# Causal attention in a Mamba and mixture-of-experts block: row maxima interleaved 20 steps ahead and placed per block of 512 queries

## The reference

```python
scores = jnp.einsum('bqhd,bkhd->bhqk', q, k) / math.sqrt(hd)      # 16 heads of width 16, 2048 tokens
scores = jnp.where(causal, scores, jnp.asarray(-1000000000.0, scores.dtype))
probs = jax.nn.softmax(scores, axis=-1)
attn = jnp.einsum('bhqk,bkhd->bqhd', probs, v).reshape(Bb, Tt, d) @ Wproj
```

## Time and profile before

| | |
|---|---|
| median of 3 runs | 4642.17 us |
| the profiled execution | 4645.66 us, its span 4644.1 us |
| busy over the span: TensorE matmul, VectorE, ScalarE, GpSimd | 79%, 61%, 53%, 41% |
| granted TensorE clock, mean | 0.858 |
| before the attention stage, 0 to 2352.7 us | TensorE busy 1736.4 us, clock 0.89 |
| attention stage, 2352.7 to 3819.8 us | TensorE busy 1360.3 us, VectorE 831.7, ScalarE 684.5, GpSimd 111.5, clock 0.83 |
| after it, 3819.8 to 4644 us | TensorE busy 549.1 us, clock 0.82 |

### The profile page before, as it was taken

How to read it: one execution, slowest core, us unless ns; L and a number is a source line. 1 busy time by engine, 2 the same in 40 slices (tenths; PEclk the granted TensorE clock), 3 DMA queues, 4 the chain that set the end, 5 groups by cost and what they waited for, 6 DMA issues and landing times. The chain is left out here.

```text
span 4644.1 us, 70787 instructions
## 1 busy us (share of the span) xinstructions
PE 3645.9 (79%) x23028; PEld 2230.4 (48%) x23028; DVE 2811.0 (61%) x4386; ACT 2476.2 (53%) x3874; POOL 1905.8 (41%) x1767
## 2 busy tenths in 40 slices
PE   8477888887878878656569999999999984499990
PEld 4156666666666666544334333333333223366660
DVE  4278888888888888644557766667657005411105
ACT  3288998889888899611201555555545431111110
POOL 0078888888888888733310010000000003300006
PEclk9689999999999999877755999999979556699995
DMA  6443333333333333344440010001000004312115
GB/s 212 116 110 83 104 98 92 83 89 96 92 83 92 83 98 96 99 160 157 170 119 3 6 20 18 18 6 20 18 8 6 8 15 148 123 62 68 70 41 182
DMA packets 163298, 367.82 MB, mean 79 GB/s; under 512 B 21603, under 2 KB 68694, under 8 KB 147984
## 3 DMA queue, kind: packets, MB, share of 16 engines
q1 hardware_dynamic: 130672, 276.91, 21.5%
q0 software_dynamic: 16784, 52.10, 3.1%
q10 hardware_dynamic: 15504, 34.61, 1.9%
HBM read 263.73 MB, written 102.26 MB: 79 GB/s over the span
## 5 line engine op out<-in xcount | busy, mean ns | idle before, releaser
L506 POOL TENSOR_TENSOR scan_hC<-scan_hh,scan_cbc 128x512 f32<-128x512 f32 x1024 | 1379.7, 1374 | 160.7 <-DVE scan_hh L718 103.9
L718 DVE TENSOR_TENSOR_SCAN scan_hh<-scan_dA,scan_state,scan_bx 128x512 f32<-128x512 f32 x1024 | 1253.1, 1265 | 212.1 <-PE scan_bx L810 102.7
L1496 PE MATMUL attend_s<-attend_kt,attend_qt 32*128 32x512 f32 (+3 forms) x2560 | 825.5, 647 | 67.3 <-DVE attend_mx L1407 28.5
L810 PE MATMUL scan_bx<-kept_ident,scan_dBxT 128*128 128x128 f32 x4096 | 678.8, 292 | 197.8 <-DVE scan_hh L718 135.0
L1515 PE MATMUL attend_s<-attend_qt,attend_kt 32*128 32x512 f32 (+3 forms) x2560 | 723.8, 652 | 8.6 <-POOL attend_pb L1380 4.1
L820 PE MATMUL scan_acc<-kept_ident,scan_hC 128*128 128x128 f32 x4128 | 657.8, 287 | 53.8 <-ACT scan_uu L568 28.3
L559 ACT ACTIVATE scan_dBxT<-scan_dtxT,scan_bt 128x512 f32<-128x512 f32 x1028 | 655.6, 710 | 81.8 <-PE scan_bx L810 81.6
L810 PEld LDWEIGHTS scan_bx<-kept_ident,scan_dBxT 128*128 128x128 f32 x4096 | 503.8, 150 | 389.6 <-DVE scan_hh L718 234.6
L1407 DVE TENSOR_REDUCE attend_mx<-attend_s 128x1 f32<-128x512 f32 x768 | 495.8, 685 | 299.1 <-PE attend_s L1496 297.3
L554 ACT ACTIVATE scan_dA<-scan_dt,scan_an 128x512 f32<-128x512 f32 x1028 | 660.9, 712 | 29.1 <-DVE scan_hh L718 29.0
L1466 ACT ACTIVATE attend_pb<-attend_s 128x1024 f32<-128x1024 f32 x384 | 390.5, 1023 | 401.7 <-PE attend_s L1515 401.7
(11 more groups left out here) (202 smaller groups left out, 3895.0 us busy)
## 6 DMA issues: line engine op xcount, KB each, us to landing
scan_xs<-scratch_xin SPq DMA_DIRECT2D x288, 256.0 KB, 6.2
scan_cbc<-scratch_crows SPq DMA_DIRECT2D x64, 1024.0 KB, 4.8
scratch_y<-scan_uu ACTq DMA_DIRECT2D x17, 1024.0 KB, 4.2
mix_yf<-scratch_y SPq DMA_DIRECT2D x10, 1024.0 KB, 5.2
mix_yb<-scratch_y SPq DMA_DIRECT2D x10, 1024.0 KB, 8.8
mix_z<-scratch_sz SPq DMA_DIRECT2D x10, 1024.0 KB, 12.5
route_at<-scratch_attn SPq DMA_DIRECT2D x160, 64.0 KB, 2.3
scratch_xin<-proj_out_x SPq DMA_DIRECT2D x8, 1024.0 KB, 5.8
```

Of the source, the lines that this page charges most:

```text
L506: pool.tensor_tensor(hC[n % 2][:, m, :], h[:, m, :], rows, ALU.mult).then_inc(hc_ok, 1)
L718: dve.tensor_tensor_scan(hh[n % 2][:, m, r], dA[n % 2][:, m, r], bx[bank(j)][:, r], state[:, d, n, m:m + 1], ALU.mult, ALU.add).then_inc(h ...
L810: last = pe.transpose(bx[bank(j)][:, t * P:(t + 1) * P], dBxT[turned_slot(n)][:, t, m * P:(m + 1) * P], k["ident"][:, :])
L1496: pe.matmul(s1[v % S1][:, 0:w], qt[n % SETS][rows, t * P:(t + 1) * P], kt_[n % SETS][rows, c * C:c * C + w], start=True, stop=True).then_i ...
```

## The change

`attend` treats units and steps as two running series over all groups, the units 20 ahead (`LEAD`). So 20 units run alone at the start, then every step has one unit beside it, of its own group or the next, and the last 20 steps have none.

The units go by block of 512 queries like the steps. In each block the four crossed units stand so that, with 20 steps between, they fall beside crossed steps of equal width where the order allows: units 20-23 beside steps 0-3, units 28-31 beside steps 8-11, the next group's units 0-3 beside steps 20-23. Units 8-11 fall beside whole steps 28-31, and steps 36-39 have whole units beside them.

The maxima are reduced, turned, copied and placed after each block, a *round*: 32 in all instead of 8, each for 16 rows of `mrows` instead of 64. VectorE copies a round's rows after the unit that follows the block. TensorE turns them at the end of the iteration with that unit, once the last tile in bank `s1[0]` has been read, and waits for the copied rows before the next tile in that bank. The second pass waits for placed maxima at the start of each block. There are two sets of `qt` and `kt_` instead of three, and the load of group n + 1 stands on the SP queue between the placements of the second and third block of group n, behind a wait for the last step of group n - 1.

In the last 20 steps the scores of both pairs follow one another on TensorE, and both halves of the values come after them.

```diff
-    SETS = 3
+    SETS = 2
     PB = 3
+    LEAD = 20
...
+    units = []
+    for qc in range(NC):
+        whole = [(t, c) for t in range(JT * qc, JT * qc + JT) for c in range(qc)]
+        crossed = [(t, qc) for t in range(JT * qc + JT - 1, JT * qc - 1, -1)]
+        at = len(whole) if qc < NC - 1 else JT
+        units += whole[:at] + crossed + whole[at:]
+    assert len(units) == NSTEP
+    NUNIT = GROUPS * NSTEP
...
-        m = s.sb("m", [P, HG, KT])
-        mrows = s.sb("mrows", [HG * KT, P])
+        m = s.sb("m", [P, HG, JT])
+        mrows = s.sb("mrows", [HG * JT, P])
...
-        pm = s1[0][0:HG * KT, 0:P]
+        pm = s1[0][0:HG * JT, 0:P]
...
-            for n in range(GROUPS):
-                place_max(n)
-                if n and n + 2 < GROUPS:
-                    load(n + 2)
+            for r in range(GROUPS * NC):
+                if r % NC == 2 and r // NC + 1 < GROUPS:
+                    load(r // NC + 1)
+                place_max(r)
...
+            def block_max(u, r):
+
+                qc = r % NC
+                dve.wait_ge(s1_read, (u + 1) * HG)
+                dve.wait_ge(edge_ok, (r + 1) * JT)
+                if r:
+                    dve.wait_ge(m_turned, r)
+                dve.tensor_reduce(m[:, :, :], mx[:, :, qc * JT:qc * JT + JT, :], AX_X, ALU.max).then_inc(m_ok, 1)
...
-            for n in range(GROUPS):
-                for st in range(NSTEP):
-                    maxima(n, st)
-                split_max(n)
-                copy_rows(n)
+            for u in range(NUNIT):
+                crossings += maxima(u)
+                if round_after(u) is not None:
+                    block_max(u, round_after(u))
+                if round_after(u - 1) is not None:
+                    copy_rows(round_after(u - 1))
+            copy_rows(GROUPS * NC - 1)
...
+                    if v % S1 == 0 and turned:
+                        pe.wait_ge(m_rows, turned)
...
-            def turn_max(n):
-                pe.wait_ge(m_ok, n + 1)
+
+            def turn_max(u, r):
+
+                last = min(u + 1, NUNIT) * HG - 1
+                pe.wait_ge(s1_read, last // S1 * S1 + 1)
+                pe.wait_ge(m_ok, r + 1)
...
-                if at % NSTEP == 0 and pair == 0:
-                    pe.wait_ge(m_in, (n + 1) * HG * 16)
+                if kt == 0 and pair == 0:
+                    pe.wait_ge(m_in, (n * NC + qc + 1) * HG * 16)
...
+            turned = 0
+            for at in range(-LEAD, NUNIT):
+                u = at + LEAD
+                if at >= 0:
+                    scores2(at, 0)
+                if u < NUNIT:
+                    scores1(u, 0)
+                    if at > 0:
+                        values(at - 1, 0)
+                if at >= 0:
+                    scores2(at, 1)
+                if u < NUNIT:
+                    scores1(u, 1)
+                elif at > 0:
                     values(at - 1, 0)
...
+                if at > 0:
                     values(at - 1, 1)
...
+                if round_after(u - 1) is not None:
+                    turn_max(u, round_after(u - 1))
+                    turned += 1
```

More of the change, by code:

```diff
@@ L1388, in _, with round_after @@
                 pool.wait_ge(stored[i], 16 * GROUPS * NC // 2)
-        def tiles1(st, heads):
-            return [(t, c, h) for t, c in firsts[st] for h in heads]
+        def round_after(u):
+            if u < 0 or u >= NUNIT or u % NSTEP not in ends:
+                return None
+            return u // NSTEP * NC + ends.index(u % NSTEP)
         @block.vector
@@ L1397, in _, with maxima @@
             dve.wait_ge(mx_ok, 1)
[L1399 to L1403, removed]
+            crossings = 0
+            def maxima(u):
+                n, (t, c) = u // NSTEP, units[u % NSTEP]
+                r = n * NC + t // JT
+                if r >= NC:
+                    dve.wait_ge(m_ok, r - NC + 1)
+                own = edge[crossings % 2]
+                for i, h in enumerate((2, 3, 0, 1)):
+                    v = u * HG + i
                     bank = s1[v % S1]
@@ new lines, in maxima @@
+                    if i == 0 and crossings >= 2:
+                        dve.wait_ge(edge_ok, crossings - 1)
+                    dve.tensor_tensor(own[:, h, :], bank[:, w:w + P], cap_s[:, :], ALU.min).then_inc(s1_read, 1)
+                if c == t // JT:
+                    dve.wait_ge(s1_read, (u + 1) * HG)
+                    dve.tensor_reduce(mx[:, :, t, JT], own[:, :, :], AX_X, ALU.max).then_inc(edge_ok, 1)
+                return c == t // JT
+            def block_max(u, r):
+                qc = r % NC
+                dve.wait_ge(s1_read, (u + 1) * HG)
+                dve.wait_ge(edge_ok, (r + 1) * JT)
+                if r:
+                    dve.wait_ge(m_turned, r)
+                dve.tensor_reduce(m[:, :, :], mx[:, :, qc * JT:qc * JT + JT, :], AX_X, ALU.max).then_inc(m_ok, 1)
@@ L1481, in _, with scores1 @@
             pe.wait_ge(caps_ok, 1)
[L1483 to L1486, removed]
+            def scores1(u, part):
+                n, (t, c) = u // NSTEP, units[u % NSTEP]
+                if u % NSTEP == 0 and part == 0:
                     pe.wait_ge(loaded[n % SETS], (n // SETS + 1) * HG * 3 * 16)
[L1488 to L1491, removed]
+                w = min(C, (t + 1) * P - c * C)
+                for i, h in list(enumerate((2, 3, 0, 1)))[2 * part:2 * part + 2]:
+                    v = u * HG + i
                     rows = slice(32 * h, 32 * h + 32)
-                    w = min(C, (t + 1) * P - c * C)
                     if v >= S1:
                         pe.wait_ge(s1_read, v - S1 + 1)
+                    if v % S1 == 0 and turned:
+                        pe.wait_ge(m_rows, turned)
                     pe.matmul(s1[v % S1][:, 0:w], qt[n % SETS][rows, t * P:(t + 1) * P],
                               kt_[n % SETS][rows, c * C:c * C + w], start=True, stop=True).then_inc(s1_mm, 1)
-                    v += 1
-            def turn_max(n):
-                pe.wait_ge(m_ok, n + 1)
+            def turn_max(u, r):
+                last = min(u + 1, NUNIT) * HG - 1
+                pe.wait_ge(s1_read, last // S1 * S1 + 1)
+                pe.wait_ge(m_ok, r + 1)
                 hold(pe, k)
```

58 lines of the change are left out of this document (14 added, 44 removed).

## The result

The changed kernel takes 4419.3 us, the median of 4 executions (4410.8 to 4420.6); the kernel before, on the same chip, 4647.0 (4641.6 to 4653.6). The ratio is 0.9506, 95% interval 0.9486 to 0.9525: 5% faster. The forecast was 4445, the range 4400 to 4510. The profiled execution took 4420.6 us, its span is 4419.1, its mean granted clock 0.89.

A forecast was written before the change was run, and what follows sets the result against it. TensorE was taken to bound the middle; VectorE and TensorE alternate in the lead. Attention: -3.5 + 76 + 2 + 1096 + 66, plus 1.5, is 1238 against 1435.5 us; 4645.7 - 197.5 - 3.5 = 4445, range 4400 to 4510.

The forecast's parts named there:

- middle: The 300 attention steps with units beside them: 7.5 groups of 146.1 us, 1096 us.
- tail: Last 20 steps, without units: four heads fill four strips; 66 us, between 60 at full clock and 74 at the lower.
- Start and lead: Before the first exponential: two memsets fewer, -3.5 us; 20 units alone instead of 40, 151.3 + 2.1 becomes 76 + 2.
- Even spread: Middle: one unit per step, none with two, -9.0 us a group; units at steps 36-39 add 0 to 0.8.
- Equal widths: Middle: crossed steps beside equally wide units take 13.0 us, steps 0-3 14.8; together -1.6 us a group.
- Rounds: Middle: turning maxima four times a group adds a transpose and two TensorE waits, 1.1 us a round, +4.4 a group.
- Whole steps: Middle: expected to stay at 3.6 us; the prediction is wrong if they grow.
- Clock: Middle: drops began around steps 36-39 and cost 4.3 us a group; 3 us a group are kept.
- Hidden rounds: Rival: transposes fit into gaps (-24), last 20 steps keep full clock (-6), crossed blocks reach 12.5 (-12); 4403 us, chance 0.12.
- Costly rounds: Rival: each round costs 2.5 us (+42) and the clock loses 5 more a group (+37); 4524 us, chance 0.12.
- clock collapse: Rival: clock falls in matched narrow blocks, 15.2 us each, 23 blocks; 4773 us, slower than before, chance 0.04.
- Late placement: Rival: nothing gained from equal widths (+12) and maxima placed late (+40); 4497 us, chance 0.04.

The follow-up runs named there:

- the lead of 30: The changed kernel with the maxima pass 30 steps ahead instead of 20 (`LEAD = 30`): 4544.4 us, ratio 0.9765 to the kernel before.
- the later turn: The changed kernel with each round's transpose moved behind the first scores of the next step: 4445.3 us, ratio 0.9555 to the kernel before.
- The edit with one wait: The changed kernel with VectorE's wait for the previous group's maxima only at each block's first unit, not every unit: 4407.9 us, ratio 0.9473.
- the repeated execution: The changed kernel, nothing changed, run once more on the chip of the follow-up runs: 4419.8 us, ratio 0.9500 to the kernel before.

## Why the prediction was right, and where its sizes were off

The sum for the profiled execution was 4645.7 - 197.5 = 4448.2 us; it took 4420.6, 27.6 less: start -2, lead +1, middle -11, tail -16.

**Start and lead.** The first scores come 5.6 us earlier for 3.5; 2.0 of it had arisen before the stage, the rest is as forecast. The lead is 79.2 for 78: right. The 4.08 us wait for the placed maxima is gone, and no such wait shows anywhere. The 10 more units alone of the lead of 30 cost 38 us, the 3.8 a unit of the prediction.

**Even spread.** Right: no step holds two units. But 0 to 0.8 for units at steps 36-39 was too little: the block takes 14.5 us for 13.4 (+8 over seven groups). The row that was read for it, of the block 20-23, does not have whole units alone beside it, though the prediction says so: 12 of its 33 first-pass matmuls are narrow.

**Equal widths.** 12.6 us for 13.0 at steps 8-11 and, before the round's share, at 20-23; 13.84 for 14.8 at steps 0-3 where the clock holds: -13 in all. The term of -1.6 a group was about half of what they are worth against the earlier trace rows, and left out that unequal steps lose more when the clock is low, which the lead of 30 showed.

**Rounds.** With the equal widths the term that was sized worst in the middle: 1.1 us a round, 4.4 a group. Against the same places in a block without a round (steps 12 and 13, 3.44 + 3.66; 8 and 9, 3.50 + 3.12), the changed kernel's group 2 has +0.68 at steps 4 and 5 (3.65 + 4.13), +0.73 at 20 and 21, +0.35 at 24 and 25, and +0.84 at 32: 2.6 in this group, and 2.9 to 3.0 in groups 1 and 3 by the same reading; about -12 in all. Both waits were real, but short: TensorE idles 5.9 us before 32 transposes and 2.3 us for the copied rows, where the prediction looked for 1 us around each. A badly placed transpose is dear for another reason, that it parts two scores that would share the array, as the later turn showed. The drain at each change of mode that the Trainium skill, "TensorEngine Tiling (Array Packing)", Key Properties, asks for has no row of its own here. A kernel without rounds wasn't tried, so 2.6 to 3.0 us is a reading of the trace.

**Whole steps.** 3.65 for 3.58 beside the units of groups 1 to 7, +9 in all on the steps without a round: not in the prediction, which went through waits added on TensorE and not those on VectorE. The edit with one wait showed it. That whole steps grow was one of the prediction's signs of being wrong; they did, by 2%.

**Clock.** 3 us a group were kept; against 13.84 for steps 0-3, which the repeated execution has where the clock held, the changed kernel lost 19 us over the 300 steps, 2.5 a group: right in size, wrong in place. The prediction took them from around steps 36-39; with units beside them these steps are at 1.00, and the falls now start in steps 0 and 1, at the stall that GpSimd's queue makes. The store stood in the same place before the change, where TensorE stood 1.71 us behind it at the start of group 2; what it cost there was not tried alone. These terms (+8, -13, -12, +9, -4) make -12, for the -11 measured. The middle came out near its 1096 also by luck: two terms that were 12 and 13 us too high stood beside 8 and 9 us that were missing.

**Tail.** 50.2 for 66, and under its lower bound of 60: the largest miss of the sum. Two terms failed. A crossed block alone takes 9.84 and 8.64 us, not 12.5: the 12.5 was read as what ScalarE and GpSimd need, but it came from the order, in which values stood between the scores of the two pairs. And a whole step is 2.64 for 2.9. The clock stays at 0.99 to 1.00, where the prediction stood halfway.

**Rivals.** *Hidden rounds* came partly true: the tail kept the full clock and crossed blocks reached 12.6, but the rounds were not hidden; the time is 16 above its 4403. *Costly rounds* and *clock collapse* are excluded, by 2.6 to 3.0 us for the four rounds of a group (10 was the rival's price) and by a mean clock of 0.97 over the 300 steps. *Late placement* shows in no row.

## What to carry to other kernels

When a packed array goes half empty, look at the granted clock of that stretch before its busy share: filling the strips won the empty strips' time and the clock. A floor read off a block is a floor only for the order it was read in. And where one engine's queue serves both computation and DMAs, look at what each DMA waits for: a store one instruction too early stalled TensorE at the start of every group here, 1.6 us a time, and the falls of the clock that went with it cost the changed kernel 19 us in one execution and 14 in another.

## What the runs showed of the hardware that was not expected

- TensorE busy 69.7 of 69.7 us with two strips of four filled: granted clock 0.50. Busy 47.4 of 52.6 with four filled: 0.99.
- With a stall of 1.9 us in step 1 the clock of steps 0-3 was 0.6 to 0.9 in all of groups 1 to 6 in one execution and in four of these six in another, where two stayed at 1.00; with a stall of 0.43 us it stayed at 1.00 in all seven groups after group 0 (group 0, which comes out of the lead at 0.50, has 0.67).
- A wait on a semaphore that has long been reached costs VectorE's loop 0.07 us a step.
- Whether the clock falls at a given place differs between executions of one kernel with the same stall in the same place.
